# Twelve of sixteen router tiles moved from between the two stages into the last steps of the first stage, and a slot table built on partitions

## The chip, the cores and the metric

One Trainium2 chip, one core. The metric is the device time of one launch in microseconds (us), lower is better. PE is the matrix engine, DVE is VectorE, ACT is ScalarE, POOL is GpSimd and SP is SyncE, which here only issues DMAs. A `q` behind an engine's name is its sequencer: the part that waits for semaphores, loads registers and hands instructions to the engine.

## What is computed

A transformer block in float32 on `x` (8, 256, 128): cross attention with 16 heads of 8 columns, then a mixture of 8 experts, of which every token takes 2. Cut to what matters:

```python
x = x + attention(layernorm(x), ctx)                     # keys: 512 of the context and 256 of its own
h = layernorm(x)
bids = sigmoid(h @ conf_w.T + conf_b) * wealth           # (8, 256, 8): the router
top_bids, selected = top_k(bids, 2)
weights = softmax(top_bids)                              # two weights for each token
expert(e, h) = (silu(h @ gate_w[e].T) * (h @ up_w[e].T)) @ down_w[e].T
x = x + sum over the two picks of weight * expert(pick, h)
```

## The kernel before

The tokens stand as 16 tiles of 128 rows (`TILES`), one token on each partition. There are two blocks with a barrier between them: `attend` and `experts`.

**`attend`** works in 32 steps `s`, called quads: four heads of one of the eight batches (`b, r = divmod(s, 4)`). Every engine goes through `step(s, b, r)` in the same order, from s = -2 to 33. In step s, DVE reduces the score maxima of quad s + 2 (six units with two PSUM pairs between PE and DVE, L463), so it has no maxima left after step 29. PE computes scores (L584), ACT their exponentials (L422), PE the weighted values (L594). DVE's `normalize(s - 1)` divides quad s - 1 by its sums, in the middle of step s. It frees a bank of a ring of three that PE needs two scores later. Once a batch, in step (b, 1), DVE adds the projected result to `m.x` (L519). POOL splits the maxima of the next quad in two parts (L338, L340), copies values, splits keys (L274, L276), and is idle for most of a step. SP's queue issues, in order, the spread of keys and of maxima.

**`experts`** begins with the router for all 16 tiles at once: statistics (L61, L65), `h` (L76), transposes and logits on PE, sigmoid, then on DVE the comparison of all pairs of bids of a token (`pair`, 128 x 1024 elements, L950 to L954). Rank below 2 is a pick. PE counts, with a triangular matrix, how many picks of the same expert stand before each (L1074, L1078), which gives every pick a row in a list sorted by expert, each expert starting at a full tile of 128. For each of the 32 pairs (pick, tile) DVE writes two one-hot matrices (`lane_hot` L989, `slot_hot` L801, 12 of these on POOL) and PE's product of them (L1089) puts the token's number at its place in a table of 128 lanes x 40 slots. From this come `source` and `target`, the row numbers for the gathers, and `table`, the expert of each slot. PE keeps running on products whose results nobody reads (`idle`, L1050).

Then 40 slots (`slots`: 8 written out, a `Fori` loop of 7 times 4, 4 written out), each a tile of 128 picks. POOL's step in slot j:

```python
pool.wait_ge(y_copied, j - 1)                    # y of slot j - 2 stands in SBUF
pool.tensor_copy(source_now[...], source[:, bass.ds(j + 4, 1)])       # L872
pool.tensor_copy(target_now[...], target[:, bass.ds(j - 1, 1)])       # L874
load((r + 3) % 4)                                # indirect DMA: the rows of slot j + 3, L855
pool.indirect_dma_start(outs_dram, ... y_out ...)                     # the rows of slot j - 2, L879
```

PE's step is gate (L1113) and up (L1116) of slot j, the transpose of x of slot j + 1 (L1105), down of slot j - 2 (L1125), and the transposes of the hidden rows of slot j - 1 (L1133). It reads the expert's number for each from `table` with `value_load` (L1099). At the end the two results of each token are loaded and added.

Of the kernel before, what the change touches and what calls it, by code (L numbers as in the profile page):

```python
# [28 lines left out]
P = 128  # L29
# [63 lines left out]
def attend(nc, m, d):  # L93
# [16 lines left out]
    with ExitStack() as ctx:  # L110
# [22 lines left out]
        proj_filled, proj_done = sem("proj_filled"), sem("proj_done")  # L133

# [19 lines left out]
        max_ps = [psum(f"max_ps{i}", 2) for i in range(2)]  # L154
        ring_ps = [psum(f"ring_ps{i}") for i in range(RING)]
        pv_ps = psum("pv_ps")
        parts_f, keys_f, blocks_f, maxT_f = [a[:].bitcast(F32) for a in (parts, keys, blocks, maxT)]
# [54 lines left out]
        def _(sp):  # L212
# [33 lines left out]
            def step(s, b, r):  # L246
# [10 lines left out]
                if 4 <= s < 4 + 2 * E:  # L257
                    e, (w, src) = (s - 4) % E, ((m.gate, "gateT"), (m.up, "upT"))[(s - 4) // E]
                    sp.dma_start(w[:, e, :], d[src][e]).then_inc(m.gate_up_in, 16)
                if has_scores(s) and s + T < QUADS:  # L260
# [9 lines left out]
        def _(pool):  # L270
# [36 lines left out]

            pool.memset(m.eps[:], EPS).then_inc(const_done, 1)
# [19 lines left out]
            def step(s, b, r):  # L328
                if has_scores(s + 1):
# [18 lines left out]
                if 0 <= b < B - 2:  # L348
# [4 lines left out]
                    if r == 3:  # L353
                        split_own(b + 2)

# [3 lines left out]
        def _(act):  # L359
# [41 lines left out]
            def step(s, b, r):  # L401
                par = s % 2
                for u in range(XUNITS):
# [30 lines left out]
            steps(step)  # L434

        @block.vector
        def _(vec):
# [46 lines left out]

            vec.memset(keys[:].bitcast(F32), -1.0).then_inc(rows_const, 1)
# [25 lines left out]
            def step(s, b, r):  # L511
                for w in range(MUNITS):
                    if has_scores(s + 2):
                        reduce_unit(s + 2, w)
                    if w == 1 and r == 1 and b >= 1:
# [5 lines left out]
                           .then_inc(proj_done, 1)  # L521
                    if w == 1 and r == 0 and 0 <= b < B - 2:
                        normalize_x(b + 2)
                    if w == 3 and 1 <= s <= QUADS:
                        normalize(s - 1)
                if has_scores(s + 2):
                    row_maxima(s + 2)
# [4 lines left out]
        def _(pe):  # L532
# [97 lines left out]

            def step(s, b, r):
                for i in range(GROUPS):
                    for a in range(2):
# [19 lines left out]
                    if i == 5:  # L653
# [4 lines left out]
                        if r == 2 and b + 2 < B:  # L658
                            project_values(b + 2)

# [3 lines left out]
class Memory:  # L664


    def __init__(self, nc, ctx):
# [5 lines left out]
        self.ident = sb("ident", [P, P])  # L673
        self.gate_up_in = ctx.enter_context(nc.semaphore("gate_up_in"))


def build(nc, d, out):
    with ExitStack() as ctx:
        m = Memory(nc, ctx)
        attend(nc, m, d)  # L680
        experts(nc, m, d, out)
# [5 lines left out]
VECTOR_SLOTS = 5 * TILES // 4  # L687
# [3 lines left out]
def experts(nc, m, d, out):  # L691


# [7 lines left out]
    with ExitStack() as ctx:  # L701
# [3 lines left out]
        ln = [sem(n) for n in ("ln2_stats", "ln2_aggr", "ln2_std", "ln2_rstd", "ln2_norm")]  # L705
        router_in, down_in, const_start, const_ready = sem("router_in"), sem("down_in"), sem("const_start"), sem("const_ready")
        ht_filled, ht_copied = sem("ht_filled"), sem("ht_copied")
        const_filled, const_copied = sem("const_filled"), sem("const_copied")
        logits_filled, logits_done, conf_done = sem("logits_filled"), sem("logits_done"), sem("conf_done")
        gap_ready, weights_done = sem("gap_ready"), sem("weights_done")  # L710
        route = sem("route")
        picks_ready, place_filled, table_ready = sem("picks_ready"), sem("place_filled"), sem("table_ready")
        mask_ready = sem("mask_ready")
        h_stored, count_consts = sem("h_stored"), sem("count_consts")
        lanes_ready, one_lane, one_slot = sem("lanes_ready"), sem("one_lane"), sem("one_slot")
        late_slot = sem("late_slot")
        picks_found, sources_ready = sem("picks_found"), sem("sources_ready")
# [11 lines left out]
        h_dram = nc.dram_tensor("h_rows", (TILES * P, C), F32, kind="Internal").ap()  # L729
# [430 lines left out]
```

## Time and profile before

| | us |
|---|---|
| median of 3 runs (535.16 to 543.32) | 541.78 |
| the profiled execution's own time | 540.74 |
| its span, first to last instruction | 539.1 |
| PE busy | 484.7 (90%) |
| DVE busy | 356.6 (66%) |
| ACT busy | 289.8 (54%) |
| POOL busy | 181.4 (34%) |

The shares are means over three stages with different limits: the attention (0 to 334), the router (334 to 377), the slots (377 to 521), and an end of 18 us. Of the slices of the page, those in which DVE and POOL are read tell more than the mean: PE is nearly always busy, also where it only runs the unread products.

### The profile page before, as it was taken

How to read it: one execution, taken by the hardware profiler on the slowest of the kernel's cores; microseconds unless marked ns; L12 is line 12 of the kernel's file. 1: busy time of each engine (PE TensorE's matmuls, PEld its weight loads, DVE VectorE, ACT ScalarE, POOL GpSimd, SP SyncE). 2: the span in 40 equal slices, each digit the busy share in tenths (PEclk: the TensorE clock that was granted, in tenths of full speed). 3: DMA queues.
4: the chain of work that ended last, by engine and by line, in shares of the span. 5: the costliest groups of instructions: out<-in, count | busy, mean ns of one | idle time of the engine just before them, and what ended most of it. 6: DMA issues, size and time to landing. Idle time of an engine off the chain costs nothing. (4 is left out here: it accounts for less than half of the span.)

```text
span 539.1 us, 10943 instructions
## 1 busy us (share of the span) xinstructions
PE 484.7 (90%) x3635; PEld 302.4 (56%) x3636; DVE 356.6 (66%) x646; ACT 289.8 (54%) x584; POOL 181.4 (34%) x381
## 2 busy tenths in 40 slices
PE   2489999999999999999999987988899999999930
PEld 1255555555555555555555544987566666666620
DVE  7798798797888887987889822589143333333316
ACT  1237777777787777777787875310133333333310
POOL 6141231412312412313200001004467666666620
PEclk9999999999999999999999998786999999999985
DMA  6512234333243343332222000800111111111126
GB/s 180 124 43 58 72 84 108 79 107 100 74 125 85 93 121 85 90 81 55 53 63 55 24 2 2 234 1 1 24 36 41 39 39 39 39 43 40 35 83 171
DMA packets 32255, 38.12 MB, mean 71 GB/s; under 512 B 5604, under 2 KB 20580, under 8 KB 32212
## 3 DMA queue, kind: packets, MB, share of 16 engines
q1 hardware_dynamic: 27252, 30.79, 21.1%
q0 software_dynamic: 2560, 5.25, 3.8%
q10 hardware_dynamic: 2400, 1.51, 1.0%
q8 instruction: 27, 0.44, 0.3%
q14 instruction: 16, 0.13, 0.1%
HBM read 16.58 MB, written 4.72 MB: 40 GB/s over the span
## 5 line engine op out<-in xcount | busy, mean ns | idle before, releaser
L463 DVE TENSOR_REDUCE max_part<-max_ps 128x2 f32<-128x1024 f32 (+1 forms) x192 | 226.0, 1221 | 39.1 <-PE max_ps L561 30.8
L422 ACT ACTIVATE probs<-ring_ps 128x512 f32<-128x512 f32 x384 | 198.4, 604 | 50.9 <-PE ring_ps L584 47.7
L584 PE MATMUL ring_ps<-blocks,keys 64*128 64x512 f32 x384 | 151.7, 473 | 2.0 <-ACT probs L422 1.5
L594 PE MATMUL pv_ps<-probs,value_cols 128*32 128x256 f32 x1536 | 103.4, 388 | 0.0
L561 PE MATMUL max_ps<-keys,blocks 64*128 64x512 f32 x256 | 84.3, 448 | 7.5 <-DMA blocks<-masked 6.4
L584 PEld LDWEIGHTS ring_ps<-blocks,keys 64*128 64x128 f32 x384 | 65.6, 187 | 31.5 <-ACT probs L422 25.2
L1018 DVE TENSOR_TENSOR hidden<-up_ps,silu 128x512 f32<-128x512 f32 x40 | 27.7, 692 | 80.9 <-PE up_ps L1116 78.7
L911 ACT ACTIVATE hiddenT<-at_ps 128x512 f32<-128x512 f32 x40 | 23.9, 597 | 75.6 <-PE at_ps L1133 67.0
L338 POOL CAST maxes<-rowmax 128x8 fp32r<-128x8 f32 x32 | 6.3, 197 | 171.2 <-DVE rowmax L470 171.2
L594 PEld LDWEIGHTS pv_ps<-probs,value_cols 128*32 128x32 f32 x1536 | 40.3, 109 | 40.2 <-issue 15.1
L561 PEld LDWEIGHTS max_ps<-keys,blocks 64*128 64x128 f32 x256 | 42.3, 196 | 26.7 <-issue 16.6
L1125 PEld LDWEIGHTS t_ps<-down,hiddenT 128*128 128x128 f32 x320 | 38.9, 192 | 14.1 <-issue 14.1
L566 PE MATMUL max_ps<-keys,blocks 64*128 64x256 f32 x256 | 44.2, 305 | 1.9 <-DVE max_part L463 1.9
L1113 PE MATMUL gate_ps<-gate,xT 128*128 x80 | 42.8, 617 | 3.2 <-DVE xT L1010 2.1
L855 POOL DMA_INDIRECT x_in<-h_rows,source_now x40 | 39.4, 986 | 17.2 <-issue 16.6
L1125 PE MATMUL t_ps<-down,hiddenT 128*128 x320 | 42.7, 277 | 2.2 <-ACT hiddenT L911 1.5
L879 POOL DMA_INDIRECT pick_outs<-y_out,target_now x40 | 39.5, 988 | 12.5 <-issue 9.2
L907 ACT ACTIVATE silu<-gate_ps 128x512 f32<-128x512 f32 x40 | 23.8, 596 | 35.1 <-PE gate_ps L1113 34.5
L1116 PE MATMUL up_ps<-up,xT 128*128 x80 | 40.9, 592 | 0.0
L566 PEld LDWEIGHTS max_ps<-keys,blocks 64*128 64x128 f32 x256 | 33.0, 195 | 12.0 <-issue 4.9
L299 POOL COPY value_cols<-ctx_v_sb 128x128 f32<-128x128 f32 x32 | 10.1, 316 | 55.4 <-PE pv_ps L594 52.4
L1050 PE MATMUL at_ps<-ident 128*128 128x128 f32 x168 | 26.5, 334 | 0.8 <-PEq L110 0.8
(150 smaller groups left out, 492.1 us busy)
## 6 DMA issues: line engine op xcount, KB each, us to landing
keys<-parts SPq DMA_DIRECT2D x96, 96.0 KB
blocks<-masked SPq DMA_DIRECT2D x93, 64.0 KB
ctx_v_sb<-ctx_v_dram SPq DMA_DIRECT2D x8, 256.0 KB, 2.9
gate<-gateT_dram SPq DMA_DIRECT2D x8, 256.0 KB, 2.8
up<-upT_dram SPq DMA_DIRECT2D x8, 256.0 KB, 2.9
y_in<-pick_outs SPq DMA_DIRECT2D x8, 256.0 KB, 5.1
raw<-ctx_kT_dram SPq DMA_DIRECT2D x7, 256.0 KB, 2.7
h_rows<-h SPq DMA_DIRECT2D x4, 256.0 KB, 5.0
```

Source lines behind the costliest of these rows:

```text
L422: act.activation(probs[par][:, k, PAIR * a:PAIR * (a + 1)], bank("exp", s * XUNITS + u)[:].rearrange("p (g n) -> p g n", n=N), ACT.Exp).th ...
L463: vec.reduce_max(out, bank, axis=AX.X).then_inc(max_done, 1)
L561: mm = pe.matmul(max_ps[w % 2][:, a * BANK:(a + 1) * BANK], blocks[rows, t, g, i * P:(i + 1) * P], keys[rows, t, 0:NC_], start=True, stop= ...
L566: mm = pe.matmul(max_ps[w % 2][:, first:first + N], blocks[rows, t, w - G, i * P:(i + 1) * P], keys[rows, t, NC_:KEYS], start=True, stop=True)
L584: pe.matmul(ps[:], keys[rows, t, k * P:(k + 1) * P], blocks[rows, t], start=True, stop=True)\
L594: mm = pe.matmul(pv_ps[ROWS * g:ROWS * (g + 1), 0:N], value_cols[:, t, k, g, :], probs[q % 2][:, k, g, :], start=(k == 0), stop=(k == KT - 1))
L855: pool.indirect_dma_start(x_in[:, r, :], None, h_dram, bass.IndirectOffsetOnAxis(ap=source_now[:, r:r + 1], axis=0))\
L879: pool.indirect_dma_start(outs_dram, bass.IndirectOffsetOnAxis(ap=target_now[:, before2:before2 + 1], axis=0), y_out[:, before2, :], None) ...
L1018: vec.tensor_tensor(hidden[:, r % 2, :], up_ps[r % 2][:], silu[:, r % 2, :], ALU.mult)\
L1113: pe.matmul(gate_ps[r % 2][:], xT[:, r % 2, :], m.gate[:, bass.ds(e, 1), :].rearrange("p a i -> p (a i)"), start=True, stop=True).then_inc ...
L1116: pe.matmul(up_ps[r % 2][:], xT[:, r % 2, :], m.up[:, bass.ds(e, 1), :].rearrange("p a i -> p (a i)"), start=True, stop=True).then_inc(up_ ...
L1125: mm = pe.matmul(y_ps[:, 0:C], hiddenT[:, r % 2, c, :], down[:, bass.ds(e, 1), c, :].rearrange("p a h -> p (a h)"), start=(c == 0), stop=( ...
```

## The change

Of the 16 tiles, 12 (`EARLY`) are routed inside `attend`.

- POOL builds the constants in step 0 (`masks`). For each batch from the second on it makes `h` of the batch before, with a power in place of ACT's root (`norm_rows`, step (b, 2)). It computes the logits of one tile in each of the steps (b, 0) and (b, 1), without PE: one product of 128 x 1024 and seven sums that halve the width (`logits`). In step 31 it does two tiles more, so that 14 have logits; the last two tiles take them from PE in `experts`.
- DVE takes the statistics of a batch behind L519 (`row_statistics`). In step 30 it computes the bids and compares 12 tiles, ahead of `normalize(29)`. In step 31 it picks, waits for PE's count, places, and writes one-hot pairs 0 to 4; behind `normalize(30)` pairs 5 to 13; in step 32 pairs 14 to 23, ahead of `normalize(31)`. A pair is now two matrices of 128 columns, since each expert has 16 fixed tiles of rows in a table of 128 lanes x 128 columns (`REACH`).
- PE counts at the start of step 31 (`count_early`, 13 products), and adds the one-hot products in three groups of 8 (`find`), at the end of step 31, in step 32 and in step 33.
- ACT computes the exponential for the early sigmoid at the start of step 30 and loads the table of the root at its end.
- SP loads the router's weights in step 2 and stores `h` by batches in steps (b, 3).
- `experts` keeps: `h` and logits of the last two tiles, and the comparison, count, placing and 8 one-hot pairs of four tiles. The number of tiles of each expert goes to POOL, which computes on partitions, one slot on each, its expert and its column of the 128. PE turns them into rows, ACT copies them to `table` and `columns`.
- In the slots POOL finds the column of a slot by loading it from `columns` with `value_load`: four times ahead of the first gather, and then twice in each step.

The core of the diff:

```diff
+def compare_tiles(vec, r, lo, hi, pair, pair2):
+    ...
+    vec.tensor_tensor(pair2, other, this, ALU.is_gt)
+    then(vec.tensor_tensor(pair, other, this, ALU.is_equal))
+    then(vec.tensor_tensor(pair, pair, r.earlier[:].unsqueeze(1).to_broadcast(pairs), ALU.mult))
+    then(vec.tensor_tensor(pair, pair, pair2, ALU.add))
+def hot_pick(vec, r, k, t, lane_hot, slot_hot):
+    vec.tensor_scalar(lane_hot, r.index[:], r.lane[:, k, t:t + 1], r.pick_id[:, k * TILES + t:k * TILES + t + 1],
+                      ALU.is_equal, ALU.mult)
+    vec.tensor_scalar(slot_hot, r.index[:], r.slot[:, k, t:t + 1], None, ALU.is_equal).then_inc(r.hot_ready, 1)
+def count_tiles(pe, r, lo, hi, ps):
+    n = hi - lo
+    pe.matmul(ps[:, 0:(n + 1) * E], r.before_r[:], r.picks[:, lo:hi + 1].rearrange("p t e -> p (t e)"), start=True, stop=False)
+    for t in range(n):
+        mm = pe.matmul(ps[:, (t + 1) * E:(n + 1) * E], r.ones_r[:],
+                       r.picks[:, lo + t, :].unsqueeze(1).to_broadcast([P, n - t, E]), start=False, stop=(t == n - 1))
...
+            def logits(t):
+                ...
+                pool.tensor_tensor(router.product[:], router.h[:, t, :].unsqueeze(1).to_broadcast([P, E, C]), router.conf_w[:], ALU.mult)\
+                    .then_inc(logit_done, 1)
+                width = C
+                for n in range(1, C.bit_length()):
+                    width //= 2
+                    pool.wait_ge(logit_done, C.bit_length() * t + n)
+                    pool.tensor_tensor(router.product[:, :, 0:width], router.product[:, :, 0:width], router.product[:, :, width:2 * width],
+                                       ALU.add).then_inc(logit_done, 1)
...
+                if r < QT and 2 <= b < B:
+                    logits(QT * (b - 2) + r)
...
+                if r == 2 and 1 <= b < B:
+                    norm_rows(b - 1)
+                if s == LAST:
+                    for t in range(QT):
+                        logits(QT * (b - 1) + t)
...
+                if s == LAST - 1:
+                    act.wait_ge(router.z_ready, EARLY)
+                    act.activation(ez[:], router.z[:, 0:EARLY], ACT.Exp, scale=-1.0).then_inc(ez_done, 1)
...
+                        row_statistics(b - 1)
...
+                    if w == 0 and s == LAST - 1:
+                        early_bids()
+                        compare_tiles(vec, router, 0, EARLY, *pair_early)
+                    if w == 0 and s == LAST:
+                        pick_tiles(vec, router, 0, EARLY, pair_early[0])
+                        vec.wait_ge(router.place_filled, 1)
+                        ...
+                        place_tiles(vec, router, 0, EARLY, router.place_ps[0], router.expert_row)
+                        early_hots(0, 5)
+                    if w == 3 and s == LAST + 1:
+                        early_hots(14, 2 * EARLY)
                     if w == 3 and 1 <= s <= QUADS:
                         normalize(s - 1)
+                    if w == 3 and s == LAST:
+                        early_hots(5, 14)
...
+            pool.wait_ge(table_ready, 2)
+            pool.wait_ge(router.h_stored, 16 * B)
             pool.wait_ge(sources_ready, 2)
 
+            def column_of(j):
+                return bass.ds(pool.value_load(columns[0:1, bass.ds(j, 1)], min_val=0, max_val=COLUMNS - 1), 1)
...
-                    pool.tensor_copy(source_now[:, r:r + 1], source[:, bass.ds(j + 4, 1)]).then_inc(source_copied, 1)
+                    pool.tensor_copy(source_now[:, r:r + 1], source[:, column_of(j + 4)]).then_inc(source_copied, 1)
...
-                    pool.tensor_copy(target_now[:, before1:before1 + 1], target[:, bass.ds(j - 1, 1)])\
+                    pool.tensor_copy(target_now[:, before1:before1 + 1], target[:, column_of(j - 1)])\
...
-                pool.tensor_copy(source_now[:, r:r + 1], source[:, r:r + 1]).then_inc(source_copied, 1)
+                pool.tensor_copy(source_now[:, r:r + 1], source[:, column_of(r)]).then_inc(source_copied, 1)
...
-            idle(20)
...
+            fill(7)
...
+            fill(12)
+            pe.wait_ge(router.picks_ready, 2)
+            count_tiles(pe, router, EARLY, TILES, router.place_ps[1])
+            fill(6)
...
+            fill(18)
```

## Rows read from the trace of the kernel before

**Rows 1.** Windows: stretch, length, busy us (and instructions) of five engines, clock, DMA
```profile
334.00:377.00 43.00, 38.48 (x229) 36.49 (x230) 33.59 (x142) 6.97 (x10) 8.85 (x28) 0.74 0.26 75
382.00:517.00 135.00, 129.69 (x672) 85.77 (x671) 47.03 (x119) 46.66 (x80) 86.00 (x152) 1.00 0.14 37
...
355.00:362.00 7.00, 7.00 (x66) 7.00 (x65) 4.96 (x18) 1.51 (x2) 0.00 (x0) 1.00 0.00 0
```

**Rows 2.** Timeline, DVE, attention's end: start, us, instruction, [idle before it and releaser]
```profile
307.96 2.36 DVE L463 TENSOR_REDUCE max_part<-max_ps 128x2 f32<-128x1024 f32 x2 [0.24 <-PE max_ps L561]
...
313.34 0.17 DVE L470 TENSOR_TENSOR rowmax<-max_part 128x8 f32<-128x8 f32 x1
...
331.78 0.23 DVE L481 TENSOR_TENSOR attn<-ring_ps,rsum 128x64 f32<-128x64 f32 x1
333.72 0.42 DVE L519 TENSOR_TENSOR x<-ring_ps,x 128x256 f32<-128x256 f32 x1 [1.72 <-PE ring_ps L617]
```

**Rows 3.** Timeline, DVE, the router
```profile
334.46 3.19 DVE L61 BATCH_NORM_STATS2 ln_stats_sb<-x 128x6 f32<-128x128 f32 x16 [0.32 <-PEq L110]
337.57 1.15 DVE L65 BATCH_NORM_AGGREGATE ln_aggr_sb<-ln_stats_sb 128x2 f32<-128x6 f32 x16
...
339.39 4.19 DVE L76 TENSOR_SCALAR h<-x,ln_aggr_sb,ln_rstd_sb 128x128 f32<-128x128 f32 x16
...
350.03 1.22 DVE L950 TENSOR_TENSOR pair<-bids 128x1024 f32<-128x1024 f32 x1
...
371.90 2.43 DVE L989 TENSOR_SCALAR lane_hot<-lane_index,lane 128x128 fp32r<-128x128 f32 x12
```

**Rows 4.** Timeline, PE, the router
```profile
334.47 7.54 PE L1050 MATMUL at_ps<-ident 128*128 128x128 f32 x40 [0.79 <-PEq L110]
...
348.78 9.02 PE L1050 MATMUL at_ps<-ident 128*128 128x128 f32 x56
...
357.70 1.89 PE L1078 MATMUL t_ps<-picks,ones_r 128*128 128x128 f32 x16
```

**Rows 5.** Timeline, POOL, the first gather and one slot of the loop
```profile
377.63 1.21 POOL L855 DMA_INDIRECT x_in<-h_rows,source_now  x1 [0.37 <-POOL source_now L884]
...
442.23 0.98 POOL L855 DMA_INDIRECT x_in<-h_rows,source_now  x1 [0.47 <-issue]
443.51 0.99 POOL L879 DMA_INDIRECT pick_outs<-y_out,target_now  x1 [0.30 <-issue]
444.63 0.18 POOL L872 COPY source_now<-source 128x1 uint32 x1
...
445.40 0.98 POOL L855 DMA_INDIRECT x_in<-h_rows,source_now  x1 [0.47 <-issue]
```

**Rows 6.** Line L1099, 443 to 444: count, ns min/median/max, first and last start
```profile
L1099 PEldq FUSED_REGOPS  x2: 42/96/151, 443.2 to 443.6; - x2
L1099 PEldq TENSOR_LOAD <-table x1: 300/300/300, 443.3 to 443.3; - x1
L1099 PEldq SEQ_ASSERT  x1: 18/18/18, 443.8 to 443.8; - x1
```

**Rows 7.** Line L870, POOL's sequencer, 442.5 to 443.3
```profile
L870 POOLq EVENT_SEMAPHORE  x1: 1767/1767/1767, 442.7 to 442.7; - x1
```

**Rows 8.** Timeline, PE, transposes of x of two slots in the loop
```profile
442.84 0.27 PE L1105 MATMUL t_ps<-ident,x_in 128*128 128x128 f32 x1
...
446.02 0.27 PE L1105 MATMUL t_ps<-ident,x_in 128*128 128x128 f32 x1
```

**Rows 9.** Chain of waits: the last indirect DMA, from its instruction to its landing
```profile
518.85 2.24 DMA pick_outs<-y_out,target_now
```

**Rows 10.** Timeline, DVE and POOL side by side at the start
```profile
6.58 4.84 DVE L452 TENSOR_SCALAR xn<-x,ln_aggr_sb,ln_rstd_sb 128x128 f32<-128x128 f32 x4
...
7.40 1.98 POOL L321 MEMSET value_cols<- 128x2208 f32 x1
```

**Rows 11.** Groups by line: POOL's subtraction of 512 columns, count, busy us, mean ns
```profile
L276 POOL TENSOR_TENSOR parts<-raw,parts 128x512 fp32r<-128x512 f32 x15 | 19.1, 1276 | 1.2
```

More of the change, by code:

```diff
@@ L110, in attend @@
+def attend(nc, m, router, d):
     with ExitStack() as ctx:
@@ L629, in _, with count_early, find @@
             pe.wait_ge(rows_const, 1)
+            def count_early():
+                pe.wait_ge(router.picks_ready, 1)
+                pe.wait_ge(masks_ready, MASKS)
+                pe.wait_ge(max_done, QUADS * MUNITS)
+                count_tiles(pe, router, 0, EARLY, router.place_ps[0])
+            def find(first, last):
+                for n in range(first, last):
+                    pe.wait_ge(router.hot_ready, n + 1)
+                    lane_hot, slot_hot = hot_of(n)
+                    mm = pe.matmul(router.found_ps, lane_hot, slot_hot, start=(n == 0), stop=False)
+                mm.then_inc(router.early_found, 1)
             def step(s, b, r):
                 for i in range(GROUPS):
+                    if i == 0 and s == LAST:
+                        count_early()
                     for a in range(2):
@@ L686, with experts @@
 PICKS = 2 * TILES * P
-VECTOR_SLOTS = 5 * TILES // 4
+COLUMNS = P + SLOTS_PAD - PICKS // P
 CHUNKS = 4
-def experts(nc, m, d, out):
+def experts(nc, m, router, d, out):
     with ExitStack() as ctx:
@@ L763, in experts @@
-        place = sb("place", [P, TILES, E])
-        row_f, row = sb("row_f", [P, 2, TILES]), sb("row", [P, 2 * TILES], I32)
-        count, full = sb("count", [P, E]), sb("full", [P, E, TILES])
-        tiles_of, first, end = sb("tiles_of", [P, E]), sb("first_slot", [P, E]), sb("end_slot", [P, E])
-        before_e = sb("before_e", [P, E, E])
-        ended, slot_e = sb("ended", [1, SLOTS_PAD, E]), sb("slot_e", [1, SLOTS_PAD])
-        table = sb("table", [1, SLOTS_PAD], I32)
+        outs_dram = nc.dram_tensor("pick_outs", (PICKS + COLUMNS * P, C), F32, kind="Internal").ap()
@@ L1002, in _ @@
[L1002 to L1005 removed]
+            then = route_chain(vec, router)
+            new = slice(TILES - NEW, TILES)
@@ new lines, in _ @@
+            vec.wait_ge(std_in, 1)
+            vec.reciprocal(router.rstd[:, 1, new], router.rstd[:, 0, new]).then_inc(rstd_in, 1)
+            vec.wait_ge(rstd_in, 1)
+            for i in range(TILES - NEW, TILES):
+                vec.tensor_scalar(router.h[:, i, :], m.x[:, i, :], router.aggr[:, i, 0:1], router.rstd[:, 1, i:i + 1],
+                                  ALU.subtract, ALU.mult).then_inc(router.norm_out, 1)
+            vec.tensor_scalar(source[:, P:], router.spare_id[:, P:], 0.0, None, ALU.mult).then_inc(sources_ready, 1)
@@ L1092, in _ @@
-            idle(24)
+            fill(7)
+            pe.wait_ge(router.norm_out, TILES)
+            for i in range(NEW):
+                mm = pe.transpose(t_ps[0][:, i * P:(i + 1) * P], router.h[:, TILES - NEW + i, :], m.ident[:])
+            mm.then_inc(ht_filled, 1)
+            pe.wait_ge(ht_copied, 1)
+            for i in range(NEW):
+                mm = pe.matmul(t_ps[1][:, i * E:(i + 1) * E], hT[:, i * P:(i + 1) * P], router.conf_wT[:], start=True, stop=True)
+            mm.then_inc(logits_filled, 1)
```

462 lines of the change are left out of this document (256 added, 206 removed).

## The prediction

> **What bounds the kernel now.** I read the windows by stage first. In the router's 43 us DVE is busy for 33.6 and each other engine does little that anybody waits for: PE's 38.5 are mostly unread products [rows 1, 4]. This stretch is one chain, from the last sum of the attention at 334.15 [rows 2] to the first gather's instruction at 377.63 [rows 5], 43.5 us. The slots follow, 40 of them in 135 us [rows 1]. Two engines are level there. PE needs 3.18 us from one transpose of x to the next [rows 8]. POOL needs 3.17 from one gather's instruction to the next, and its own pieces fill that: 0.98 gather, 0.30 gap, 0.99 scatter, 0.13, the two copies (0.30 from the start of the first to the end of the second), 0.47 to the next gather [rows 5]. POOL's 66% share on the page is a mean; here it has nothing to spare. In the attention PE is full, and DVE waits a few tenths before most pairs of maxima [rows 2].
>
> The sum is made against the profiled execution, 540.74 us with a span of 539.1. The median of 541.78 lies 0.2% above it, so the difference is carried over as it is.
>
> **Part 1, the attention up to step 30.** DVE gets two statistics and two aggregates for each batch: 2 x 0.20 and 2 x 0.07 [rows 3] and two semaphore waits, 0.7 us, seven times. Against them stand DVE's waits of 0.24 and the like [rows 2], so most is hidden and I charge 0.15 each time, 1 us (bounds 0 and 5, all seven in full). POOL gets the logits of a tile. A product of 512 columns takes 1.28 [rows 11]; I take 2.3 for 1024, and 1.3, 0.7, 0.5, 0.3 and four of 0.2 for the sums and the bias, with waits 6.7 us. That fits into a step of some 8.6 to 10 us in which POOL works little, but ends just before the maxima that POOL has to split next. Queued behind it are that split and the copies of values; both have a step's slack or more. DVE's `xn` in four steps now meets POOL's product; 0.25 each, 1 us. SP's store of `h` waits for `norm_out`, with the spread of keys behind it, but `norm_rows` is a step earlier: nothing. Sum of part 1: +2, bounds 0 and 6.
>
> **Part 2, the tail of the attention.** After 313.5 DVE had only three `normalize` and one sum [rows 2]. Now, in its order: ACT's exponential ahead, 0.4; three small steps, 0.8; four comparisons of 768 elements, 0.75 x 1.22 = 0.95 each, 3.9 with the waits [rows 3]; the reduction and seven small steps, 2.8; a wait for PE's count, 13 products at 1.89/16 = 0.12 plus the way there and back, 1.7 [rows 4]; placing, 9 steps at about 0.28, the mean of the 18 steps between 355 and 362 [rows 1], 2.4; 24 one-hot pairs at 0.26 for the form with two scalars (4.19/16) and 0.20 for the other (2.43/12) [rows 3], 11.0; three `normalize`, 1.4. That is 24.4, so `normalize(31)` ends near 337.9 in place of 332.0 [rows 2]. From there to the last sum it is 2.1 as before (332.0 to 334.15), then 0.7 of statistics. PE's finds lie beside DVE's pairs or beside the sum. The block ends near 340.8 in place of 334.15, +6.6. DVE and POOL disturb each other: at 6.58 four `xn` took 4.84 us, where sixteen of the same form take 4.19 later, and a fill of POOL of 1.98 us ran through them [rows 10, 3]. In the tail POOL's `logits(12)` and `(13)` lie beside DVE's comparisons and pairs. This delays `normalize(29)`, which PE's ring needs, and then all behind it. I take +1.9 for it (bounds 0 and 8), and the tail is +8.5: `experts` starts near 343, or 345 with part 1.
>
> The Trainium skill, SBUF — State Buffer, section "Who interferes with whom", says more: a DVE instruction with two SBUF inputs, or in a mode with two ports, excludes POOL's and the reverse, for the whole instruction. The stretched `xn` agrees. By that rule the four comparisons, too, would take turns with POOL's products; this is the second rival below.
>
> **Part 3, what stays of the router.** From the start of `experts`: seven unread products at 0.38 (7.54/20 turns) [rows 4], 2.6, longer than the root, reciprocal and two `h` (1.6), so PE's filler sets the time; transposes, copy, eight-column products, bias and sigmoid on three engines, 2.2 with the hops; bids 0.3; comparison of 256 elements, four at 0.42, 1.7; reduction and picks 0.6. Then PE's twelve fillers (0.32 each, 9.02/28 [rows 4], 3.9 from the logits) are about done. Count 0.9, tiles of each expert 0.6, placing 1.6, eight pairs 3.7, last product and `source` 1.1. With 0.8 for semaphores this is 16.1. POOL's table (some 13 small steps, 3.4 us, beside DVE's pairs), PE's two products and ACT's two copies are late by about the same: 16.6. Then the value loads ahead of the first gather. On PE's sequencer one goes from 443.2 to 443.8 with a load of 0.30 in it [rows 6]; I take 0.7 and 0.15 for the copy, four times 3.4, and 0.4 to the gather [rows 5]. Sum 20.4 against 43.5: -23.1 (bounds -25 and -20.5, for fillers at full clock or a table 2.5 later). Parts 2 and 3 together bring -14.6. The 2 MB of down weights are issued 2.5 us into this chain of 20, beside it, and I take nothing for them. PE's granted clock, 0.74 on the mean of this stretch before [rows 1], I leave as the fillers' rows have it.
>
> **Part 4, two value loads in each slot.** No trace here shows one on POOL. The bounds are nothing and 2 x 0.7 = 1.4 us a slot, 38 slots, 0 and +53. What hides them: POOL's sequencer runs ahead of its engine. It stood at its wait from 442.7 on [rows 7], while the gather of 442.23 ran and the scatter of 443.51 was only queued [rows 5]. But it stood there for 1.77 us, until 444.47, when y was copied, just as the scatter ended at 444.50. So with today's timing nothing would be hidden. POOL then falls behind y, and what it is behind is what it hides. It may fall behind until x comes late: from a gather's instruction at 442.23 to the transpose at 446.02 it is 3.79 [rows 5, 8]; landing 2.24 [rows 9] and 0.35 for the weights leave 1.2. So 1.2 of 1.4 are hidden, and the remaining 0.2 are shared, since a longer slot gives two slots' more slack: 0.1 a slot, +4. I take this since it is nearest to what rows 7 show, a sequencer ahead of a queued instruction.
>
> **Sum.** +2 (part 1) + 8.5 (part 2) - 23.1 (part 3) + 4 (part 4) = -8.6. From 541.78 this is 533, 1.6% faster. A change within 2% (531 to 552.6) is about what a measurement of this kernel can't tell from none.
>
> **The rivals.**
> - *The loads are exposed* (ends slower). If a queued copy holds the sequencer, so that the second load of a step can't run before the first copy has, or if a load waits for the engine, one load of 0.7 or both stay open. Against it: rows 7. For it: there the sequencer passed a DMA, not a copy, and loaded nothing. Price for one: 38 x 0.7 = 27 in place of 4, 556; for both 53, 582. It decides from 0.34 us a slot on, where 12.6 + 0.4 from parts 1 to 3 are used up. Chance 0.18.
> - *DVE and POOL take turns.* If each of four comparisons waits for a product of POOL (2.3, 1.3, 0.7 and so on), `normalize(29)` comes 3 us late, the pairs lose 3 more to `logits(13)`, and the attention's `xn` and split 3: +8, 541. Chance 0.15.
> - *All is hidden.* No disturbance in the tail (-1.9), nothing in part 1 (-2), value loads free (-4): 525. For it: every part has a cover in the rows. Chance 0.27, as anything from 522 to 531.
> - The change could move the router and gain nothing because another chain, POOL's table, is last. Its 3.4 us and the way over PE and ACT can at most be 3 later than `source`: 536, in the forecast's range.
>
> **Chances.** Forecast 0.40, with its own range 529 to 538. The fast rival and the forecast's lower edge give 0.38 for faster by over 2%; exposed loads 0.18 for slower; the rest, 0.44, within 2%. The range reaches from 524 to 550: it leaves out 0.03 below and most of the exposed loads above.
>
> **What would show it.** First gather's instruction near 365 in place of 377.63 (parts 1 to 3 right), the block's barrier near 345 (parts 1 and 2), the last maxima near 315.5 in place of 313.34 (part 1). In the loop, a distance of 3.25 to 3.4 between gathers; POOL's wait at the line of L870 should have shrunk to nothing, and the value loads should start while a scatter runs. If they start only when it has ended, and the distance is 3.9 or 4.6, the first rival is right. Stretched comparisons in step 30 beside long POOL products would show the second. The prediction is wrong mainly if the value load on POOL costs something else than on PE, or if the sequencer can't run it ahead.

## The result, and the profile after

The changed kernel takes 550.55 us (median of 4, 547.43 to 552.03), the kernel before beside it 540.97 (535.16 to 543.32): ratio 1.0206, 95% interval 1.0108 to 1.0304. It is slower, beyond the noise; whether by more than 2% the interval leaves open. The forecast was 533, with 550 as the upper end of its range. The profiled execution took 550.12, with a span of 548.1 against 539.1.

The windows, router and slots, against [rows 1]:

```profile
349.00:370.80 21.80, 19.03 (x96) 16.97 (x96) 11.22 (x53) 4.07 (x9) 4.18 (x19) 0.66 0.36 103
380.00:515.00 135.00, 126.69 (x609) 77.77 (x607) 42.69 (x108) 43.63 (x73) 81.85 (x139) 1.00 0.12 34
```

The router's stretch is halved. In the same 135 us of slots every engine did less: PE 609 products in place of 672, POOL 139 instructions in place of 152. The slots are slower, and no engine is fuller.

DVE in the timeline, at one of the four steps with a product of POOL beside `xn`, and at the attention's end, against [rows 2]:

```profile
113.73 2.00 DVE L621 TENSOR_SCALAR xn<-x,ln_aggr_sb,ln_rstd_sb 128x128 f32<-128x128 f32 x2
...
316.94 0.17 DVE L639 TENSOR_TENSOR rowmax<-max_part 128x8 f32<-128x8 f32 x1
...
319.26 0.95 DVE L118 TENSOR_TENSOR xn<-bids 128x768 f32<-128x768 f32 x1
...
323.86 0.82 DVE L128 TENSOR_SCALAR picks<-rank 128x96 fp32r<-128x96 f32 x1
324.60 1.43 DVE L130 TENSOR_SCALAR top<-rank 128x96 f32<-128x96 f32 x2
...
329.31 2.29 DVE L152 TENSOR_SCALAR lane_i<-row 128x24 int32<-128x24 int32 x1
331.51 0.17 DVE L153 TENSOR_SCALAR slot_i<-row 128x24 int32<-128x24 int32 x1
331.71 1.23 DVE L154 CAST slot<-slot_i 128x24 f32<-128x24 int32 x1
...
347.80 0.42 DVE L715 TENSOR_TENSOR x<-ring_ps,x 128x256 f32<-128x256 f32 x1 [2.48 <-PE ring_ps L829]
```

POOL in the same stretch:

```profile
318.77 3.15 POOL L446 TENSOR_SCALAR h<-x,ln_aggr_sb,ln_rstd_sb 128x128 f32<-128x128 f32 x2
321.89 2.72 POOL L453 TENSOR_TENSOR product<-h,conf_w 128x1024 f32<-128x1024 f32 x1
...
329.19 2.37 POOL L453 TENSOR_TENSOR product<-h,conf_w 128x1024 f32<-128x1024 f32 x1 [0.17 <-POOL z L462]
```

`lane_i` has 24 elements for each partition and took 2.29 us. It began 0.12 after POOL's product at 329.19 and ended 0.04 after that product's end at 331.56. The same form with the same 24 elements, at 331.51, took 0.17.

POOL's timeline at the first gather, against the first row of [rows 5]:

```profile
369.35 0.18 POOL L1104 COPY source_now<-source 128x1 uint32 x1 [0.47 <-issue]
370.01 0.18 POOL L1104 COPY source_now<-source 128x1 uint32 x1 [0.48 <-issue]
370.82 1.26 POOL L1075 DMA_INDIRECT x_in<-h_rows,source_now  x1 [0.62 <-POOL source_now L1104]
```

And two slots of the loop, against the others of [rows 5]:

```profile
471.86 0.99 POOL L1099 DMA_INDIRECT pick_outs<-y_out,target_now  x1 [0.30 <-DVE y_out L1202]
472.85 0.19 POOL L1092 COPY source_now<-source 128x1 uint32 x1
473.19 0.18 POOL L1094 COPY target_now<-target 128x1 uint32 x1
473.85 0.99 POOL L1075 DMA_INDIRECT x_in<-h_rows,source_now  x1 [0.48 <-issue]
475.14 0.99 POOL L1099 DMA_INDIRECT pick_outs<-y_out,target_now  x1 [0.30 <-issue]
476.62 0.18 POOL L1092 COPY source_now<-source 128x1 uint32 x1 [0.50 <-issue]
477.36 0.18 POOL L1094 COPY target_now<-target 128x1 uint32 x1 [0.55 <-issue]
478.01 0.99 POOL L1075 DMA_INDIRECT x_in<-h_rows,source_now  x1 [0.48 <-issue]
```

In the first slot the loads ran beside the scatter, and the two copies follow it, 0.34 apart. In the second they did not, and 0.74 lies between the starts of the copies. What the sequencer did there, by line, from 474 on, where [rows 7] had its one wait (at L1090 the wait for y ends, which the trace puts together with the wait for a store; L1072 is the value load):

```profile
L1072 POOLq TENSOR_LOAD <-columns x2: 287/289/291, 475.9 to 476.7; - x2
...
L1090 POOLq EVENT_SEMAPHORE  x1: 1502/1502/1502, 474.3 to 474.3; - x1
```

The wait ends at 475.83, and only then come the loads, the first at 475.94: they stand behind the wait in the program. From y copied to the gather's instruction it is now 2.2 to 2.5 us, before it was 0.9 to 1.06.

The first slot tells something else. Its second load:

```profile
L1072 POOLq TENSOR_LOAD <-columns x1: 294/294/294, 472.5 to 472.5; - x1
```

It began at 472.51, beside the scatter and ahead of the first copy, which stands before it in the program and ran only at 472.85. So neither a running DMA instruction nor a queued copy holds the sequencer's loads here.

PE, too, has a load behind a wait. Its waits for x from 380 to 515 (total, times, longest), which in the kernel before were 0.8 us in 2:

```profile
PEld t_ps L1260 <- DMA x_in<-h_rows,source_now: 7.2, 13, 1.3
```

And its timeline after one such wait, against [rows 8]; the sequencer's load (L1254) for the down product (L1280) began at 473.3, when x had come:

```profile
473.47 0.27 PE L1260 MATMUL t_ps<-ident,x_in 128*128 128x128 f32 x1
474.22 1.04 PE L1280 MATMUL t_ps<-down,hiddenT 128*128 x7 [0.47 <-issue]
```

At 470.00, where x had been early, the down product followed 0.11 after the transpose. Here it is 0.75.

The sum, in both profiled executions:

| | before | after | difference | forecast |
|---|---|---|---|---|
| last maxima (part 1) | 313.34 | 316.94 | +3.6 | +2 |
| from there to the block's end (part 2) | 20.8 | 32.0 | +11.2 | +8.5 |
| to the first gather (part 3) | 43.5 | 21.9 | -21.6 | -23.1 |
| first gather to first transpose | 4.16 | 3.98 | -0.2 | 0 |
| first to last transpose of x (part 4) | 127.5 | 143.8 | +16.3 | +4 |
| to the end | 29.8 | 29.5 | -0.3 | 0 |

### The profile page after: what moved, and what is told of

Read it like the earlier page. It is cut to its first block and busy times, and to the rows that moved or that the text cites. A ratio compares the mean times of both kernels' runs of the same rounds, so it can differ in the third digit from the quotient of the medians.

```text
span 548.1 us, 11191 instructions
## 1 busy us (share of the span) xinstructions
PE 481.1 (88%) x3514; PEld 288.6 (53%) x3515; DVE 369.1 (67%) x665; ACT 290.2 (53%) x586; POOL 284.8 (52%) x539
## 5 line engine op out<-in xcount | busy, mean ns | idle before, releaser
L632 DVE TENSOR_REDUCE max_part<-wide 128x2 f32<-128x1024 f32 (+1 forms) x192 | 225.6, 1218 | 34.6 <-PE wide L773 29.0
L773 PE MATMUL wide<-keys,blocks 64*128 64x512 f32 x256 | 84.5, 449 | 7.6 <-DMA blocks<-masked 6.5
L1194 DVE TENSOR_TENSOR hidden<-wide,silu 128x512 f32<-128x512 f32 x40 | 27.7, 692 | 86.4 <-PE wide L1271 82.2
L773 PEld LDWEIGHTS wide<-keys,blocks 64*128 64x128 f32 x256 | 42.3, 196 | 26.9 <-issue 16.7
L459 POOL TENSOR_TENSOR product<-product 128x512 f32<-128x512 f32 (+6 forms) x98 | 49.1, 501 | 7.7
L1280 PE MATMUL t_ps<-down,hiddenT 128*128 x320 | 44.5, 282 | 7.5 <-issue 5.9
L1280 PEld LDWEIGHTS t_ps<-down,hiddenT 128*128 128x128 f32 x320 | 38.9, 191 | 21.3 <-issue 21.3
L778 PE MATMUL wide<-keys,blocks 64*128 64x256 f32 x256 | 46.2, 310 | 4.2 <-DVE max_part L632 4.2
L1268 PE MATMUL wide<-gate,xT 128*128 x80 | 44.2, 634 | 4.4 <-DVE xT L1186 2.7
L1099 POOL DMA_INDIRECT pick_outs<-y_out,target_now x40 | 39.5, 987 | 12.9 <-issue 5.8
L778 PEld LDWEIGHTS wide<-keys,blocks 64*128 64x128 f32 x256 | 34.4, 196 | 15.0 <-DVE max_part L632 8.6
L1271 PE MATMUL wide<-up,xT 128*128 x80 | 40.8, 592 | 0.0
L1131 ACT ACTIVATE silu<-wide 128x512 f32<-128x512 f32 x40 | 23.9, 598 | 30.4 <-PE wide L1268 27.0
L453 POOL TENSOR_TENSOR product<-h,conf_w 128x1024 f32<-128x1024 f32 x14 | 33.6, 2402 | 0.2 <-POOL z L462 0.2
```

The lines of the kernel that those rows point to most:

```text
L459: pool.tensor_tensor(router.product[:, :, 0:width], router.product[:, :, 0:width], router.product[:, :, width:2 * width], ALU.add).then_in ...
L632: vec.reduce_max(out, bank, axis=AX.X).then_inc(max_done, 1)
L773: mm = pe.matmul(max_ps[w % 2][:, a * BANK:(a + 1) * BANK], blocks[rows, t, g, i * P:(i + 1) * P], keys[rows, t, 0:NC_], start=True, stop= ...
L778: mm = pe.matmul(max_ps[w % 2][:, first:first + N], blocks[rows, t, w - G, i * P:(i + 1) * P], keys[rows, t, NC_:KEYS], start=True, stop=True)
L1099: pool.indirect_dma_start(outs_dram, bass.IndirectOffsetOnAxis(ap=target_now[:, before2:before2 + 1], axis=0), y_out[:, before2, :], None) ...
L1268: pe.matmul(gate_ps[r % 2][:], xT[:, r % 2, :], m.gate[:, bass.ds(e, 1), :].rearrange("p a i -> p (a i)"), start=True, stop=True).then_inc ...
```

## The experiments

All times are beside runs of the kernel before on the same chip (its medians: 539.97, 540.1 and 540.47 in the three groups, 540.97 beside the changed kernel). The changed kernel itself was not run again in these groups, so a difference from its 550.55 can be off by about 1 us. "A slot" is the mean distance from the ninth to the last transpose of x in the profiled execution: 3.31 in the kernel before, 3.74 in the changed one. Stretches and starts come from one profiled execution of each kernel.

### The slots: POOL's loads

**Both loads ahead of the step's waits.** The changed kernel, with `column_of` called before the waits of the step:

```diff
+                source_col = column_of(j + 4) if exists(i, r, 4) else None
+                target_col = column_of(j - 1) if exists(i, r, -1) else None
                 if exists(i, r, 3):
                     pool.wait_ge(xT_filled, j + 1)
...
-                    pool.tensor_copy(source_now[:, r:r + 1], source[:, column_of(j + 4)]).then_inc(source_copied, 1)
+                    pool.tensor_copy(source_now[:, r:r + 1], source[:, source_col]).then_inc(source_copied, 1)
```

> The changed kernel, with both value loads of POOL's step placed ahead of the step's waits, so that they run while the gather and the scatter before them do. Theory (exposed loads close a ring): from y's copy to the next gather it was 2.2 us in place of 0.98, x then came late, and PE, made to wait for x, had its own value load for the down product behind that wait. Ahead of the waits the loads are hidden: 0.98 to 1.1 again, 3.3 us a slot in place of 3.74, T39 - T0 near 128 in place of 143.8, total 534 to 536. Rival (the loads cost POOL's time wherever they stand, or the slots are slower for the new banks of PSUM and code): at most 0.1 us a slot comes back, total 546 to 550.

533.02, ratio 0.9892 (0.9855 to 0.993). First to last transpose 130.4, 3.32 a slot, from y to the gather 1.06 to 1.4. A slot of POOL:

```profile
458.41 0.99 POOL L1101 DMA_INDIRECT pick_outs<-y_out,target_now  x1 [0.30 <-issue]
460.00 0.18 POOL L1094 COPY source_now<-source 128x1 uint32 x1 [0.60 <-DVE y_out L1204]
460.13 0.17 POOL L1096 COPY target_now<-target 128x1 uint32 x1
460.77 0.99 POOL L1075 DMA_INDIRECT x_in<-h_rows,source_now  x1 [0.47 <-issue]
```

The loads are the same and as many, and the time is 17.5 us less, 13.4 of them from the first to the last transpose in the two profiled executions (the profiled execution of this run also had a start 2.0 us shorter, with the clock granted in full 4.6 us earlier). What costs is not the load, but its place behind the wait. This run doesn't test the first rival's queued copy, since both loads now stand ahead of both copies; the load at 472.51 above does, and excludes it.

**One and two loads put into the kernel before**, whose results nobody reads, behind the waits (the first kernel has only the first of the two new lines; both also wait once for `table` ahead of the slots):

```diff
                 if exists(i, r, 4):
+                    pool.value_load(table[0:1, bass.ds(j + 4, 1)], min_val=0, max_val=E - 1)
                     pool.tensor_copy(source_now[:, r:r + 1], source[:, bass.ds(j + 4, 1)]).then_inc(source_copied, 1)
                 if exists(i, r, -1):
+                    pool.value_load(table[0:1, bass.ds(j - 1, 1)], min_val=0, max_val=E - 1)
```

> The kernel before, with one value load (of a number that is not used) ahead of the first copy in POOL's step. Theory of the ring with a threshold: y's copy to gather 0.98 + 0.65 = 1.6 us; the ring of two slots is then 1.5 + 1.6 + 2.75 = 5.85 us, below PE's 2 x 3.16 = 6.32, so nothing is lost but a few tenths at the loop's ends: 541 to 543. Rival (each load costs what it takes, 38 x 0.65): 565. Rival (half of what two loads cost, in proportion): 549.

545.3, ratio 1.0114 (1.0045 to 1.0183); 3.49 a slot.

> The kernel before, with two such value loads, one ahead of each copy. Theory: ring 1.5 + 2.25 + 2.75 = 6.5 us, above 6.32, PE waits for x and then pays for its own value load each time: 3.74 us a slot, +16, total 556 to 559. Rival (the slots of the changed kernel are slower for another reason than the loads): 541 to 546.

555.21, ratio 1.0304 (1.0242 to 1.0367); 3.74 a slot, 142.2 from first to last transpose: the changed kernel's slots, without its router. The loads alone give 14.7 of the 16.3 us of part 4.

One load already costs 6.6 us of these 14.7, 0.18 a slot. A few tenths in all were expected, since a load of 0.65 fits into the slack of 1.2. The trace with one load shows why. From a gather to the down product two steps on (POOL, PE's sequencer by line, PE, PE):

```profile
468.40 0.98 POOL L856 DMA_INDIRECT x_in<-h_rows,source_now  x1 [0.48 <-issue]
L1101 PEldq TENSOR_LOAD <-table x1: 429/429/429, 471.1 to 471.1; - x1
471.54 0.27 PE L1107 MATMUL t_ps<-ident,x_in 128*128 128x128 f32 x1
472.08 1.15 PE L1127 MATMUL t_ps<-down,hiddenT 128*128 x8 [0.27 <-issue]
```

PE did not wait for x: the transpose follows the up product at once. But PE's sequencer waits for x too, and its own load for the down product stands behind that wait. It began 2.65 after the gather, and the down product came 0.54 after the transpose, where 0.11 is usual. In the kernel before, the down product came more than 0.12 after the transpose in 2 slots of 37, with one load in 13. Such a late down product starts 3.4 to 3.7 after the gather's instruction in most cases, and in the kernel before the gather was 3.75 or more ahead of the transpose, 3.86 ahead of the down product. So the slack was some 0.2 to 0.5 us, an estimate from these rows, and not 1.2, and one load is more than that. The run that would test this reading, PE's load ahead of its wait in the kernel with one load, was not made.

**PE's load ahead of its wait for x**, in the changed kernel:

```diff
+                e_down = expert(j - 2) if exists(i, r, -2) else None
                 if exists(i, r, 1):
                     transpose_x(i, r, 1)
                 if exists(i, r, -2):
-                    e = expert(j - 2)
+                    e = e_down
```

> The changed kernel, with PE's value load of the expert for the down product moved ahead of the wait for x. POOL's loads stay exposed. Theory (the second half of the ring's price is PE's value load behind a wait that now waits): T to the copy of y returns from 1.9 to 2.4 us to 1.5, the ring is 6.5, the slot 3.3 to 3.4, total 537 to 541. Rival (POOL's loads alone make the slot long): total stays 548 to 551.

538.87, ratio 0.9988 (0.9952 to 1.0024); 3.48 a slot. From y to the gather it is still 2.2 to 2.5, and PE waits for x 30 times in place of 13, 15.6 us in all. Yet 10 us of the slots are gone: a late x no longer makes the down product late, so y comes 1.5 to 1.8 after the transpose and not 1.5 to 2.4.

**Both together.**

> The changed kernel with the two edits of the slots alone: both value loads of POOL ahead of its step's waits, and PE's value load for the down product ahead of its wait for x. Theory: both lie on the same ring of one slot (y copied, gather, x, transpose), so they add up until PE's own 3.16 us a slot is the bound: a mean slot of 3.2, 40 slots in 126.7 in place of 143.8, and the time is 3.5 us under the 533.0 of POOL's edit alone: 528.5 to 530.5. Rival: once POOL is early, x lands before PE asks, and PE's edit is worth nothing: 532.5 to 533.5 and 3.32 a slot.

528.85, ratio 0.9789 (0.9741 to 0.9836); 3.22 a slot, first to last transpose 125.1. PE's timeline:

```profile
442.35 0.27 PE L1262 MATMUL t_ps<-ident,x_in 128*128 128x128 f32 x1
442.46 1.06 PE L1283 MATMUL t_ps<-down,hiddenT 128*128 x8
...
445.55 0.27 PE L1262 MATMUL t_ps<-ident,x_in 128*128 128x128 f32 x1
```

Both together bring 21.7 us, POOL's edit alone 17.5 and PE's alone 11.7: they work on the same ring and share 7.5. The slots are now 2.4 us shorter than those of the kernel before, which has PE's load behind the wait too; that edit alone was not tried on it.

### The attention

**xn away from POOL's product.**

```diff
-                    if w == 1 and r == 0 and 0 <= b < B - 2:
-                        normalize_x(b + 2)
+                    if w == 0 and r == 3 and -1 <= b < B - 3:
+                        normalize_x(b + 3)
```

> The changed kernel, but DVE normalises x of batch b + 3 (four steps xn) in step (b, 3), where POOL has no product of 1024 columns, in place of batch b + 2 in step (b, 0). Theory: the attention's loss of 3.6 us (last maxima at 316.94 in place of 313.34) is made only by these four xn meeting POOL's logits in steps (2, 0) to (5, 0); then the last maxima come at 313.4 to 314 and the time falls by 2.5 to 3.6 us, to 547 to 548. Rival: the loss is made by the DVE's statistics or by POOL's later copies and splits; then the last maxima stay near 317 and the time at 550.5.

548.62, ratio 1.0151 (1.0087 to 1.0214). From the tenth to the eleventh set of maxima 8.58 in place of 9.44, as in the kernel before (8.58), and so in all four steps. But the last maxima came at 316.1, so neither expectation was met: from the first maxima to the third it took 18.98 in place of 16.82, and the clock was granted in full only from 47.0 on, in place of 43.9. I had moved the first xn into the ramp, ahead of step 0.

> The changed kernel, but xn of batches 3 to 7 moved to the steps (b, 3), from (0, 3) on; xn of batch 2 stays in step (0, 0), which the earlier form of this edit had moved into the ramp ahead of step 0. Theory: the steps (2, 0) to (5, 0) lose nothing (8.6 us in place of 9.4) and the ramp is as in the changed kernel, so the last maxima come at 313.0 to 313.8 and the time is 546.5 to 547.5. Rival: the later rise of the clock in that run (46.7 to 47.0 in place of 44) had nothing to do with xn of batch 2; then it is there again, the last maxima at 316 and the time at 548.5 to 549.5.

545.77, ratio 1.0121 (1.007 to 1.0171). Last maxima 312.48, the four steps 8.58 each. The ramp was 15.64, shorter than in the changed kernel, with the clock full from 41.5. Ramps of 14.9 to 16.8 stand in the profiles of kernels whose ramp is the same, and two of 19.0 in the two that have xn there. So the four steps' 3.4 us are shown. That xn of batch 2 costs 2.2 in the ramp rests on two executions.

**The logits of tiles 12 and 13 to PE.** Four transposes and four products in the second block in place of two each:

```diff
-                if s == LAST:
-                    for t in range(QT):
-                        logits(QT * (b - 1) + t)
...
-            for i in range(NEW):
+            for i in range(LATE):
                 mm = pe.matmul(t_ps[1][:, i * E:(i + 1) * E], hT[:, i * P:(i + 1) * P], router.conf_wT[:], start=True, stop=True)
```

> The changed kernel, but the logits of tiles 12 and 13 are left to PE in the second block (four transposes and products there in place of two), so that POOL has no work beside DVE's picks and pairs in step 31. Theory: the seven small DVE steps that took 0.7 to 2.3 us each beside POOL's logits fall to 0.1 to 0.3, some 5 us of DVE's time; normalize(30) comes that much earlier and PE's wait of 3.7 us for it nearly goes. The last sum of x comes 4 to 5.5 us earlier than 347.80, at 342.5 to 344; the second block grows by 0.5 to 1; the time is 546 to 547.5. Rival: the tail is DVE's own work of pairs and waits, and POOL has nothing to do with it; then the last sum stays within 1 us of 347.80 and the time is 550 to 552.

546.74, ratio 1.0167 (1.0082 to 1.0252). DVE's timeline:

```profile
317.73 0.95 DVE L118 TENSOR_TENSOR xn<-bids 128x768 f32<-128x768 f32 x1
...
326.52 0.18 DVE L152 TENSOR_SCALAR lane_i<-row 128x24 int32<-128x24 int32 x1
...
330.68 0.21 DVE L643 RECIPROCAL rsum<-ring_ps 128x8 f32<-128x8 f32 x1 [1.21 <-PE ring_ps L812]
...
342.64 0.42 DVE L712 TENSOR_TENSOR x<-ring_ps,x 128x256 f32<-128x256 f32 x1 [2.47 <-PE ring_ps L826]
```

`lane_i` takes 0.18. From the last maxima to the last sum it is 27.2 in place of 30.9, so 3.6 us of the tail were POOL's doing. DVE itself needed 6.0 less up to `normalize(30)`; of these 2.3 came back as waits for PE, 1.13 for the count and 1.21 ahead of `normalize(30)`. The second block up to the first gather took the same (23.1 and 23.0 from the last sum). The comparison at 319.26 took 0.95 with and without POOL's logits; those began only at 321.89, beside the last of the four, so the two had hardly met.

**The first five pairs behind `normalize(30)`**, `early_hots(0, 14)` there in place of (0, 5) ahead and (5, 14) behind.

> The changed kernel, but the first five one-hot pairs come behind normalize(30) in place of ahead of it, with pairs 5 to 13. Theory: PE's wait of 3.7 us for normalize(30) falls to about 1.5, since the five pairs took 2.3 us ahead of it, but DVE is the tail's bound, with the same work, so the last sum moves by less than 1 us: 346.8 to 348. The granted clock of PE may fall later. Rival: what counts is PE's stop and the half clock after it; without the stop the products of find and the last scores run at full clock, and the last sum comes 2 to 3 us earlier.

549.22, ratio 1.0186 (1.0127 to 1.0244). The step of `normalize(30)` that writes `attn` came 16.3 after the last maxima in place of 19.1, the last sum 30.5 after them in place of 30.9. DVE's amount of work sets the tail, not its order. The clock says the same: PE's fell to half at 337.5 in the changed kernel and at 326.0 in the first experiment, and from the last maxima to the last sum both took 30.9.

### All together

> The changed kernel with four edits at once: both value loads of POOL ahead of its step's waits, PE's value load of the down product ahead of its wait for x, xn moved to step (b, 3), and the logits of tiles 12 and 13 left to PE. Theory: the edits are in different stretches and add up, POOL's and PE's loads apart, which work on the same ring: 533.0 for the first, less 3 for xn, less 4 for the tail, and 0 to 4 for PE's load: 522 to 526.5, and under the kernel before by 2.5 to 3.4%. A mean slot of 3.18 to 3.32 us. Rival: the gains cover each other (DVE's order in the attention is set by PE), and it stays above 529.

532.92, ratio 0.9854 (0.9784 to 0.9924): 6 us over the slow end of what was expected. The slots are as expected (126.7, 3.22 each). The ramp was 18.97 (the xn in it). And the tail took 30.8 although POOL's logits are out of it. The window with PE's clock (last but two), and, in the timeline, what DVE waited for:

```profile
327.00:340.00 13.00, 12.68 (x71) 5.70 (x74) 8.42 (x39) 5.41 (x11) 0.00 (x0) 0.50 0.00 1
```

```profile
333.76 0.21 DVE L643 RECIPROCAL rsum<-ring_ps 128x8 f32<-128x8 f32 x1 [4.00 <-PE ring_ps L812]
```

Once DVE has less to do, PE sets the tail, and in this execution it was granted 0.5 from 326.6 on; in the run with the logits alone it kept 1.0 up to 338.1. From the last sum to the first gather it then took 26.0 in place of 23.1.

**Five edits**: the xn of batch 2 back in step (0, 0), and five pairs put where DVE waits 2.5 us for PE, in step 32:

```diff
                     if w == 3 and s == LAST + 1:
-                        early_hots(14, 2 * EARLY)
+                        early_hots(14, 19)
                     if w == 3 and 1 <= s <= QUADS:
                         normalize(s - 1)
...
+                    if w == 3 and s == LAST + 1:
+                        early_hots(19, 2 * EARLY)
```

> The changed kernel with five edits: the two of the slots, xn of batches 3 to 7 in the steps (b, 3), logits of tiles 12 and 13 left to PE, and one-hot pairs 19 to 23 behind normalize(31), where DVE waits 2.5 us for PE in every profile. Theory: under the 532.9 of the four edits by 2.7 (ramp) and 2 (pairs), 527 to 529 if PE's clock falls to half at 326 again, in which case the tail waits for PE (4.00 us ahead of normalize(30)); 522 to 525 if it falls after 337 as in the run with the logits alone. Rival: the tail is PE's at half clock anyway and the pairs bring nothing: 530 to 531.

523.8 (five runs from 521.75 to 524.61, one of 530.76), ratio 0.9691 (0.9649 to 0.9733). The clock fell at 335.3. The last sum came without a wait, 25.0 after the last maxima, and the first gather at 360.32:

```profile
334.98 0.23 DVE L647 TENSOR_TENSOR attn<-ring_ps,rsum 128x64 f32<-128x64 f32 x1
...
337.65 0.42 DVE L712 TENSOR_TENSOR x<-ring_ps,x 128x256 f32<-128x256 f32 x1
```

This kernel is 3.1% faster than the kernel before, and some 27 us under the change as it came, with the same idea. It rests on this kernel as a whole; the gain of the five pairs was not measured by itself.

**And unread products in PE's gaps**, one at three places of each of the steps 30 to 33:

```diff
+                    if s >= LAST - 1 and i in (1, 3, 5):
+                        if s == LAST - 1 and i == 1:
+                            pe.wait_ge(max_done, QUADS * MUNITS)
+                        pe.matmul(m.wide[1][:, BANK:BANK + P], m.ident[:], m.ident[:], start=True, stop=True)
```

> The five edits and, in the steps 30 to 33, one unread product of 128 columns on PE at each of three places ahead of weighted values, where PE waits 0.2 to 0.5 us for ACT's exponentials. Theory: PE's granted clock falls at 326 because PE has gaps from 315 on (2.48 busy of 3); with the gaps filled it falls later or not at all in the tail, and the time is 2 to 5 us under the five edits without it. Rival: the fills are too few or their place is wrong; the clock falls as before and the time is the same or 0.5 us more.

521.93 (520.84 to 527.35), ratio 0.969 (0.9641 to 0.9739): the same. Its window, where the five edits without it had 10.61 us of PE at 0.82:

```profile
327.00:340.00 13.00, 12.03 (x103) 8.03 (x103) 10.86 (x49) 6.18 (x12) 0.00 (x0) 1.00 0.01 1
```

The clock stayed full until 354.7. From the last maxima to the last sum it took 26.8 in place of 25.0, from there to the first gather 21.0 in place of 22.7. So with the products in its gaps PE kept the full clock longer than in any profile without them (341.4 at the latest), in one execution. The tail still became no shorter: DVE waited 2.04 for PE ahead of `normalize(30)` in place of 1.19.

## Why the prediction was wrong

**The step that failed is in part 4**: "POOL then falls behind y, and what it is behind is what it hides", with 0.1 us a slot as its result. Measured 0.43, 16.3 us in place of 4. Those 12.3 are two thirds of the miss of 17.6. Two things in it were wrong.

The first is the slack. The 1.2 took the landing of 2.24 from [rows 9], which is a scatter's, and counted nothing for PE's own value load between x and the down product. With both in it, it was 0.2 to 0.5 us, by the traces of the kernel before and of the one with one load.

The second is that I took y's time as given. The down product that makes y stands behind the transpose of a later x, and so behind a gather: from the gather of slot j + 1 to the down product of slot j - 2, from there to y of slot j - 2, from y to the gather of slot j + 3. This ring spans two slots. An estimate from the traces with late down products: 3.65 (the median, PE's load in it), 1.5, and 2.3 with two loads of POOL, 1.6 with one and 1.1 with the loads ahead of the waits. That is 7.45, 6.75 and 6.25, or 3.7, 3.4 and 3.1 a slot, against 3.16 to 3.20 that PE needs by itself. Measured were 3.74, 3.49 and 3.32, and 3.31 in the kernel before, where no load of POOL is in the ring: the slot of 3.18 from which I started was one of its shorter ones. The profile before showed PE's wait for x only twice, so I didn't look at what stood behind it. The experiments took out the one load (3.32), the other (3.48), both (3.22), and rebuilt the 3.74 in the kernel before.

The first rival had the right side, exposed loads, but another mechanism and too high a price: not a queued copy, but the semaphore wait ahead of the loads holds the sequencer, and it cost 16.3 us and not 27 for one load exposed. It was to decide from 0.34 us a slot on; with parts 1 to 3 as they came it did so from 0.18 on (6.8 over 38 slots).

**Part 1**, +2 against +3.6: the term of xn was mis-sized, 0.25 each where it was 0.85, four times. Statistics, at 1 us, cost nothing: up to the tenth set of maxima both kernels took the same (81.67 and 81.66).

**Part 2**, +8.5 against +11.2. The pairs (11.0 forecast, 24 x 0.455 = 10.9) and comparisons (3.9 with waits) held. With POOL out of the tail, DVE went from the last maxima to the end of `normalize(31)` in 24.8, against my 24.4. What was mis-sized is the disturbance: 1.9 forecast, 3.6 by the experiment, and its place: not `normalize(29)` and comparisons, but the smallest steps behind them. From the end of `normalize(31)` to the end of the last sum it took 2.9, not 2.1.

**Part 3**, -23.1 against -21.6: 20.4 forecast and 21.9 measured, in a stretch with the granted clock at 0.66. The four loads cost 0.65 to 0.66 each, near the 0.7 taken from PE. No run tells which term was short. The starting value of 43.5 wasn't firm either: the same instructions took 40.8 in the profiles with one and two loads added, with a mean clock of 0.79 in place of 0.74.

**The second rival** (DVE and POOL take turns, +8 over all) was right in kind and stood in the wrong place. The comparisons kept 0.95 to 1.09 beside POOL's two `h`, and it was these that took longer, 3.15 where the same two took 1.58 at 285.58. By the Trainium skill, SBUF — State Buffer, section "Who interferes with whom", only the shared port pair contends, and it is an exclusive lock. The trace of `lane_i`, which ended 0.04 after POOL's product, agrees: an instruction's own length says nothing of how long it may wait.

Parts 1 to 3 together brought -6.8 in place of -12.6. With the slots as forecast that would have been some 3 us faster than before, within the range.

## What to carry to other kernels

A value load stands in program order behind every wait of its engine. Put it ahead of the step's waits, above all ahead of the wait for the buffer that closes a ring; in this kernel that was 17.5 us at no cost in work, 13.4 of them measured in the slots. Before calling a delay hidden by lateness, follow the ring round: if what the engine waits for depends on its own earlier output, lateness hides nothing beyond the ring's slack. And count in that slack what the other engines' sequencers have yet to do once their wait ends, even where the engines themselves never wait. When work moves beside another engine's, look at the smallest instructions, since each can wait a whole instruction of the other.

## What was not expected of the hardware

- A DVE step of 24 elements took 2.29 us beside a POOL product of 2.37, and 0.17 without one.
- A value load of one number from SBUF took 0.29 us on POOL's sequencer and 0.30 to 0.44 on PE's; with its address and bounds, 0.65 to 0.74 from one to the next.
- PE's granted clock fell to 0.5 at 326 to 328 in four profiles of variants of the changed kernel, and at 332 to 341 in six others, over nearly the same instructions. In five of the six PE was in a wait of 3.2 to 3.7 us or just behind it; in the four it had had none longer than 0.52 since 312. With an unread product in PE's small gaps the fall came at 354.7, in one execution.
- The ramp at the start, from the first maxima to the third, varied from 14.9 to 16.8 us with the time at which the clock was granted in full (39.3 to 44.4).
